# Cross attention: the context is turned on VectorE in 32 by 32 blocks laid out by the transfers, not on TensorE; ScalarE adds the value bias

## What is computed

```
q = (layernorm(x) @ wq.T + bq), k = (ctx @ wk.T + bk), v = (ctx @ wv.T + bv)   # D = 512, 16 heads of 32
scores = q k^T / sqrt(32);  attn = softmax(scores);  ctx_out = attn @ v
x = x + ctx_out @ wo.T + bo
```

## Time and profile before

| | |
|---|---|
| time, median of 3 runs | 1736.51 us (1735.48 to 1738.24) |
| time of the profiled execution | 1736.3 us |
| its span, first to last instruction | 1734.1 us |
| TensorE busy | 1665.6 us, 96% |
| VectorE busy | 1178.3 us, 68% |
| ScalarE busy | 933.3 us, 54% |
| GpSimd busy | 645.9 us, 37% |
| transfers, mean rate | 51 GB/s |

### The profile page before, as it was taken

How to read it: one execution, slowest core, us unless ns; L and a number is a source line. 1 busy time by engine, 2 the same in 40 slices (tenths; PEclk the granted TensorE clock), 3 DMA queues, 4 the chain that set the end, 5 groups by cost and what they waited for, 6 DMA issues and landing times. The chain is left out here.

```text
span 1734.1 us, 37329 instructions
## 1 busy us (share of the span) xinstructions
PE 1665.6 (96%) x16084; PEld 1365.8 (79%) x16084; DVE 1178.3 (68%) x1555; ACT 933.3 (54%) x1405; POOL 645.9 (37%) x352
## 2 busy tenths in 40 slices
PE   7999999999999999999999999868899899999999
PEld 6788888888888888888888888656787677778787
DVE  5137887878788878878787888787633577753322
ACT  4236666666676666666666766654201677731000
POOL 0003555555555555555555545202000144432210
PEclk9999999999999999999999999878899899899999
DMA  5211101011110101010111100213323111211001
GB/s 194 66 42 35 41 30 43 29 41 42 30 42 29 43 29 41 31 43 29 41 38 35 41 29 8 76 47 114 128 85 104 50 56 45 74 51 46 28 25 49
DMA packets 73283, 88.74 MB, mean 51 GB/s; under 512 B 6912, under 2 KB 39680, under 8 KB 73120
## 3 DMA queue, kind: packets, MB, share of 16 engines
q1 hardware_dynamic: 73120, 86.36, 15.5%
HBM read 71.67 MB, written 14.68 MB: 50 GB/s over the span
## 5 line engine op out<-in xcount | busy, mean ns | idle before, releaser
L638 POOL TENSOR_TENSOR b_acc<-b_acc,b_s 128x1024 f32<-128x1024 f32 x168 | 459.0, 2732 | 258.1 <-ACT b_s L846 247.5
L875 DVE TENSOR_TENSOR b_s<-b_s,b_mb 128x2048 f32<-128x2048 f32 x128 | 365.5, 2857 | 3.9 <-ACT b_mb L829 3.9
L913 DVE TENSOR_TENSOR b_mx<-b_psS,b_mx 128x512 f32<-128x512 f32 x480 | 331.1, 690 | 52.4 <-PE b_psS L710 39.2
L846 ACT ACTIVATE b_s<-b_s 128x2048 f32<-128x2048 f32 x128 | 245.2, 1916 | 82.2 <-DVE b_s L875 82.2
L855 ACT ACTIVATE b_s<-b_psS 128x2048 f32<-128x2048 f32 x128 | 240.8, 1881 | 69.7 <-DVE b_mx L913 69.7
L43 PE MATMUL b_work<-wvT,cT 128*128 128x512 f32 x496 | 203.1, 409 | 0.0
L43 PE MATMUL b_work<-cT,wkT 128*128 128x512 f32 x496 | 200.3, 404 | 0.0
L45 PE MATMUL b_work<-wvT,cT 128*128 128x512 f32 x496 | 194.2, 391 | 0.0
L45 PE MATMUL b_work<-cT,wkT 128*128 128x512 f32 x496 | 193.7, 390 | 0.0
L44 PE MATMUL b_work<-wvT,cT 128*128 128x512 f32 x496 | 193.5, 390 | 0.0
L44 PE MATMUL b_work<-cT,wkT 128*128 128x512 f32 x496 | 193.5, 390 | 0.0
(11 more groups left out here) (291 smaller groups left out, 2845.1 us busy)
## 6 DMA issues: line engine op xcount, KB each, us to landing
cin<-in_ctx SPq DMA_DIRECT2D x64, 512.0 KB, 3.4
experts_sb<-in_L_ffn_expert_w SPq DMA_DIRECT2D x8, 1024.0 KB, 5.3
q_scratch<-d_st SPq DMA_DIRECT2D x16, 256.0 KB, 2.3
k_scratch<-d_st SPq DMA_DIRECT2D x16, 256.0 KB, 2.3
e_q<-q_scratch SPq DMA_DIRECT2D x16, 256.0 KB, 2.7
k_sb<-k_scratch SPq DMA_DIRECT2D x16, 256.0 KB, 2.9
b_kT<-in_x SPq DMA_DIRECT2D x4, 512.0 KB, 8.3
q_scratch<-a_q SPq DMA_DIRECT2D x8, 256.0 KB, 2.3
```

The source lines that it names most:

```text
L638: nc.gpsimd.tensor_tensor(acc[:, :, :], acc[:, :, :], s[:, buf, 2 * i:2 * i + 2, :], ALU.add).then_inc(sum_done, 1)
L846: nc.scalar.activation(part, part, ACT.Exp, scale=SCALE).then_inc(exp_done, 1)
L875: nc.vector.tensor_tensor(s[:, n % BUFS, :, :], s[:, n % BUFS, :, :], mb[:, :].rearrange("p (o n) -> p o n", o=1).broadcast_to([P, CHUNK, ...
L913: nc.vector.tensor_tensor(mx[:, :, :], part, mx[:, :, :], ALU.max).then_inc(mx_done, 1)
```

## The change

TensorE no longer turns the context of the chunks 2 to 31. A unit is now 128 features (k) of a chunk of 512 tokens. SP loads it with four transfers, one for each 32 features, each into 32 partitions of `cin`: within a partition lie 16 runs of 32 numbers (128 bytes), so that the 32 x 32 blocks already stand at their final place and only each block has to be turned in itself. VectorE does that with one instruction of 128 x 512 (`nc.vector.transpose`) from one half of `cin` to the other. ScalarE and VectorE then make the high and low half from `cin` in SBUF, where they read PSUM before. A unit is turned in the beat in which the unit before it is split, and its load is issued when the unit two before it has been turned. The turned blocks leave the ring of banks. Apart from that, ScalarE adds the value bias, after the exponential of its beat.

```diff
+def load_blocks(sp, ctx_in, cin, raw_in, p, k):
+    rows = ctx_in[p // 4, (p % 4) * 512:(p % 4 + 1) * 512, k * P:(k + 1) * P]
+    blocks = rows.rearrange("(t j) (i c) -> i j t c", j=32, i=4)
+    for i in range(4):
+        sp.dma_start(cin[32 * i:32 * i + 32, 0, k % 2, :].rearrange("j (t c) -> j t c", c=32),
+                     blocks[i]).then_inc(raw_in[k % 2], 16)
...
+            sp.wait_ge(full, place["c", 1, 1] + 1)
+            for k in range(2):
+                load_blocks(sp, ctx_in, cin, shared.raw_in, 2, k)
...
+            return None if n is None or n < 2 * CHUNK else divmod(n, CHUNK)
+        def turned_next(beat):
+            return transposed(beat + 2)
...
-            if (x0 := transposed(beat)) is not None:
-                enter(("T", *x0), beat)
...
+            sp.wait_ge(turned, 1)
+            load_blocks(sp, ctx_in, cin, shared.raw_in, 2, 2)
             for beat in range(FIRST, LAST):
...
+                if (x0 := turned_next(beat - 1)) is not None and x0[0] * CHUNK + x0[1] + 2 < SLOTS * CHUNK:
+                    u = x0[0] * CHUNK + x0[1]
+                    sp.wait_ge(turned, u - 2 * CHUNK + 1)
+                    load_blocks(sp, ctx_in, cin, shared.raw_in, *divmod(u + 2, CHUNK))
...
             for beat in range(FIRST, LAST):
-                if (x0 := transposed(beat)) is not None:
-                    transposes(*x0)
...
+                    act.wait_ge(turned, (p - 2) * CHUNK + k + 1)
+                    nc.scalar.activation(cT[0][:, p % 2, k, :], cin[:, 1, k % 2, :], ACT.Copy).then_inc(hi_done, 1)
...
+                if (m := normal_slot(beat)) is not None:
+                    g = m % G
+                    act.wait_ge(od_free, m + 1)
+                    if m >= 2:
+                        act.wait_ge(o_out[m % 2], 16 * (m // 2))
+                    nc.scalar.activation(o_st[:, m % 2, :], oq[:, :], ACT.Identity,
+                                         bias=bv[:, g:g + 1]).then_inc(o_done, 1)
...
+            def context_turned(p, k):
+                u = (p - 2) * CHUNK + k
+                dve.wait_ge(shared.raw_in[k % 2], 16 * 4 * (u // 2 + 1))
+                reached(dve, split_done, u - 2 + 2 * CHUNK + 1 if u >= 2 else 0)
+                nc.vector.transpose(cin[:, 1, k % 2, :], cin[:, 0, k % 2, :]).then_inc(turned, 1)
...
+            context_turned(2, 0)
...
-                    nc.vector.tensor_scalar(o_st[:, m % 2, :], oq[:, :], bv[:, g:g + 1], None,
-                                            ALU.add).then_inc(o_done, 1)
...
+                    nc.vector.tensor_tensor(cT[1][:, p % 2, k, :], cin[:, 1, k % 2, :], f32(cT[0][:, p % 2, k, :]),
+                                            ALU.subtract).then_inc(split_done, 1)
+                if (x0 := turned_next(beat)) is not None:
+                    context_turned(*x0)
```

More of the change, by code:

```diff
@@ L119, in __init__ @@
         self.cin_in = [sem(f"cin_in{i}") for i in range(2)]
+        self.raw_in = [sem(f"raw_in{i}") for i in range(2)]
         self.x_in = sem("x_in")
@@ L291, in _ @@
             load_weights(2)
[L292 to L295, removed]
+            for h in range(2):
+                sp.wait_ge(full, place["c", 0, 2 * h + 1] + 1)
+                load_context(1, h)
+            sp.wait_ge(full, place["c", 1, 1] + 1)
+            for k in range(2):
+                load_blocks(sp, ctx_in, cin, shared.raw_in, 2, k)
             for n, (_, half, g) in enumerate(order_of["q"]):
@@ L526, in value_places @@
             return [first + g * step for g in range(G)]
-        ident, cT, v, cin_in = shared.ident, shared.cT, shared.v, shared.cin_in
+        ident, cT, v = shared.ident, shared.cT, shared.v
         wkT, wvT = shared.wkT, shared.wvT
@@ L547, in cross_attention @@
         const = sem("b_const")
+        turned = sem("b_turned")
         bias_in = sem("b_bias_in")
@@ L652, in wait_evicted @@
                     kind, m, n = unit
-                    if kind == "T":
-                        pe.wait_ge(split_done, m * CHUNK + n + 1)
-                    elif kind == "K":
+                    if kind == "K":
                         pe.wait_ge(k_done, m * CHUNK + n + 1)
@@ L666, in bank_of @@
                 return work[BANK[unit]]
[L668 to L677, removed]
             def keys(p, g):
@@ L834, in _ @@
                 if (x0 := transposed(beat)) is not None:
[L835 to L838, removed]
+                    p, k = x0
+                    act.wait_ge(turned, (p - 2) * CHUNK + k + 1)
+                    nc.scalar.activation(cT[0][:, p % 2, k, :], cin[:, 1, k % 2, :], ACT.Copy).then_inc(hi_done, 1)
                 if (m := spread_slot(beat)) is not None:
@@ L879, in _ @@
                 if (m := normal_slot(beat)) is not None:
-                    g = m % G
                     if m == SLOTS - 1:
@@ L892, in _ @@
                     dve.wait_ge(rd_done, m + 1)
+                    reached(dve, o_done, m)
                     nc.vector.tensor_tensor(oq[:, :], psO[:, 0:P], rD[:, :], ALU.mult).then_inc(od_free, 1)
-                    dve.wait_ge(od_free, m + 1)
-                    if m >= 2:
-                        dve.wait_ge(o_out[m % 2], 16 * (m // 2))
-                    nc.vector.tensor_scalar(o_st[:, m % 2, :], oq[:, :], bv[:, g:g + 1], None,
-                                            ALU.add).then_inc(o_done, 1)
-                if (x0 := transposed(beat)) is not None:
-                    p, n = x0
-                    dve.wait_ge(hi_done, p * CHUNK + n + 1)
-                    nc.vector.tensor_tensor(context_place(cT[1], p, n), two(work[BANK["T", p, n]]),
-                                            f32(context_place(cT[0], p, n)), ALU.subtract).then_inc(split_done, 1)
+                if (x0 := transposed(beat)) is not None:
+                    p, k = x0
+                    dve.wait_ge(hi_done, p * CHUNK + k + 1)
+                    nc.vector.tensor_tensor(cT[1][:, p % 2, k, :], cin[:, 1, k % 2, :], f32(cT[0][:, p % 2, k, :]),
+                                            ALU.subtract).then_inc(split_done, 1)
+                if (x0 := turned_next(beat)) is not None:
+                    context_turned(*x0)
                 if (n := score_step(beat)) is not None:
```

1 line of the change is left out of this document (removed).

## The result

The changed kernel takes **1722.13 us** (median of 4 runs, 1721.59 to 1723.19) beside 1736.17 (median of 4, 1735.48 to 1738.24) for the kernel before: a ratio of 0.9916, 95% interval 0.9903 to 0.9928. It is faster by 14.0 us, where 11.6 were forecast (1724.9). The profiled spans are 1734.1 and 1720.6 us, 13.5 apart, so the trace holds nearly all of it.

The account below looks back on a forecast made before the run. TensorE was taken to set the pace of a 34.10 us slot. The first 15 units give 6.5 us, 27 later slots of 0.2 give 5.1: 11.6 off 1736.5, so 1724.9 us (range 1680 to 1742; main case 1714 to 1736).

Parts of the forecast that it names:

- step 3: Chunk 1's split waits for GpSimd's second add, until 19.7 us; chunk 2's scores come at 25.3, TensorE stands still 1.5.
- the circle: The forecast's walk through one steady slot, closing on itself from chunk 3's scores to the next: 33.9 us, 0.2 less.
- step 1: Slot's start: subtraction of the maximum, wanted at 7.98 us, waits for GpSimd's adds until 8.2 and is over at 10.3.
- step 2: Split, turn, maxima and ScalarE's move follow; TensorE starts chunk 1's scores at 16.4 us, with no loss yet.
- step 4: GpSimd's add of chunk 0 holds the split where it held the bias; split over at 28.2 us, scores moved at 33.6.
- step 6: GpSimd's adds of chunk 1 run 28.2 to 33.1 us; the last subtraction ends 1.25 into the next slot.
- The first 15 units: Beats 8 to 36, before GpSimd works in full: TensorE gives back 0.43 us per unit, 6.5 us.
- rival (b): The turn is long and stands twice in the slot's chain: at 1.26 us (two passes) 1759 us; chance 16%.
- (a): The split after chunk 1's scores isn't held by the port: slot 32.4 us, 52 us gained, 1684 us; chance 18%.
- (c): GpSimd's adds fall 0.2 to 0.4 us later than in the circle, eating the gain: 1732 to 1742 us; chance 10%.
- (d): Context transfers are late, above 66 ns per small packet; at 80 ns 216 us more, 1941 us; chance 4%.
- (e): TensorE's clock might be granted at less than full; expected busy 96%, so left out, with no chance given.

Follow-up runs that it names:

- Experiments 1 and 2: GpSimd's adds cut to 8 of 512 columns, most sums left out: in the changed kernel 1688.66 us, in the kernel before 1737.40 us.
- experiment 3: Changed kernel with the split's subtraction (low half of the context) replaced by an equally long instruction with one SBUF input: 1687.38 us.
- experiment 5: Changed kernel with each of GpSimd's adds in two halves of 128x512, all sums kept: 1696.19 us.
- experiment 11: Changed kernel with GpSimd's adds in halves and ScalarE copying the high half one beat earlier for all but a part's first unit: 1696.18 us.
- experiment 4: Changed kernel with every turn made twice, one right behind the other: 1766.32 us.
- Experiment 9: Changed kernel with context loads in rows of 2 KB in place of 128-byte pieces, the layout in blocks left out: 1723.85 us.
- experiment 7: Changed kernel with the value bias back on VectorE: 1725.41 us.
- experiment 10: Changed kernel with GpSimd's adds in quarters of 128x256, same sums: 1696.98 us.

## Why the prediction was right, and where its terms were off

**The port, step 3: right, and shown.** The forecast said that the new split, not the turn, decides the result, since GpSimd's second add has waited and takes the port first. In times from the scores of chunk 3 (560.40), the trace beside the circle:

| event | forecast | measured |
|---|---|---|
| step 1: subtraction over | 10.3 | 570.57: 10.2 |
| step 2: scores of chunk 1 | 16.4 | 576.79: 16.4 |
| step 3: the pair of adds over | 19.2 | 579.51: 19.1 |
| step 3: split over | 19.7 | 579.99: 19.6 |
| step 3: scores of chunk 2 | 25.3 | 585.50: 25.1 |
| step 4: split over | 28.2 | 588.35: 28.0 |
| step 5: scores of chunk 3 | 33.9 | 594.15: 33.75 |

TensorE stands still for 8.71 - 7.38 = 1.3 us, forecast 1.5. Experiments 1 and 2 show that the adds are the cause and only in the changed kernel, 3 that it is the split's second input, 5 that the length of one hold is what counts. Of the Trainium skill (SBUF — State Buffer, "Who interferes with whom") the rule that two SBUF inputs contend and one doesn't agrees with experiment 3 (2.48 against 0.69 at the same place inside the pair of adds); the trace also agrees with its sentence that the shared port is an exclusive lock (the split is over 0.48 us after the add, not before).

**The size of a slot's gain: right in kind, off by half.** Forecast 34.1 to 33.9, measured 34.11 to 33.74: 0.37 in place of 0.2. The circle is 0.15 too long (0.2 with the unrounded 25.3 + 8.65 = 33.95), and all of it lies before the scores of chunk 2, since the 8.65 behind them were exact. About 0.1 is step 1. By step 6 the last subtraction should have ended 1.25 into the next slot; the split at 561.48 shows 1.08. GpSimd's adds for chunk 2 were then over at 563.59 + 4.86 = 568.45, the subtraction at 568.37 met the tail of them and took 2.28, unheld, and through ScalarE's exponential GpSimd's pair of step 3 was over earlier too. The rest is rounding in the chain behind it: from the split's end to the scores of chunk 2 it took 585.50 - 579.99 = 5.51, not 5.6. The sum itself was loose: 27 x 0.2 is 5.4, and with 33.95 it is 27 x 0.15 = 4.1; the recorded 5.1 lies between. With a gain that is the difference of two numbers near 34, 0.15 is nearly its whole size: 5.1 became 9.6.

**The first beats: the wrong term.** "The first 15 units give 15 x 0.43 = 6.5 us" measured 4.0. What failed is the assumption that TensorE alone sets the pace there. Up to the first scores it held: they come at 103.33 in place of 106.33, though TensorE's first instruction of the stage came at 70.48 in place of 70.20. So the 7 units up to there gave 3.3, or 0.47 each. The 8 behind them gave 1.0 in place of 3.4. (Together 4.3, of which the later start takes 0.3.) First TensorE, then VectorE of the changed kernel in those beats:

```profile
103.33 1.17 PE L709 MATMUL b_psS<-b_q,b_kT 32*128 32x128 f32 x32
...
110.81 1.17 PE L709 MATMUL b_psS<-b_q,b_kT 32*128 32x128 f32 x32 [0.63 <-ACT b_s L860]
```

```profile
104.68 0.69 DVE L911 TENSOR_TENSOR cT<-cin,cT 128x512 fp32r<-128x512 f32 x1 [4.12 <-ACT cT L835]
105.29 0.70 DVE L871 STREAM_TRANSPOSE cin<-cin 128x512 f32<-128x512 f32 x1
105.92 0.65 DVE L920 COPY b_mx<-b_psS 128x512 f32<-128x512 f32 x1
```

The scores start at 103.33, but VectorE first waits for the high half, splits and turns, and looks at them only 2.6 us later, at 105.92 (before it was 106.33 to 107.82, 1.5). Of these 1.1 more 0.63 are the turn. The maxima take 2.8 more and ScalarE's move 1.9, and TensorE waits for it, four times among these beats for 0.3 to 0.6 us, 2.0 in total, most of the missing 2.4. TensorE got faster, and the chain of scores, maxima and move took over. The port has no part in it: from the first reduction of turned maxima to the second it is 30.56 us with the adds and 30.54 with the small ones of experiment 1. An early high half (experiment 11) gave only 0.4 us of the 2.4 back, so the split's wait for the high half, ahead of the maxima, is at most a part; how the rest divides stays open. The two misses are of opposite sign (+4.5 and -2.5). That the forecast of 11.6 came as close to 14.0 as it did is luck; its terms were off by more.

**The turn, rival (b): right.** The 120 turns take 695 to 712 ns, and what follows starts 0.63 after their start (105.29 to 105.92). So does the one at 588.35, 0.70 inside a pair of GpSimd's adds (588.23 to 593.15). No second pass over four bytes shows (it would have been 1.26). The Trainium skill's 311 ns for a two-byte 128 x 128 block (VectorE: DVE Perf Modes, "The three transpose paths") can't be held against it: no run here turns two-byte data. The price of a longer turn (0.2 us per slot for 0.1) came out in experiment 4, though by another chain.

**The other rivals.** (a) The split not held: it would have given 1684; the two kernels in which it isn't held gave 1687 and 1689. Its slot, 32.4, was exact, and its 6.5 us for the first beats are most of what is missing. (c) The gain eaten: not here, the adds fell 0.15 earlier than in the circle (568.45 - 560.40 = 8.05, forecast 8.2), not later. Its time of 1732 to 1742 doesn't follow from its own terms either: 0.2 to 0.4 us for each of 27 slots, added to 1724.9, is 1730 to 1736. (d) Transfers: 310240 packets at 21.7% of 16 engines and 1720.6 us are 19 ns each in the mean, far below the 59 of the bound. VectorE waited once for a context load, 1.1 us, at its third turn. Experiment 9 settles it. The warning of the Trainium skill (DMA: Bandwidth & Descriptors, "Specifications") shows in the packets' time and landing, but not in the kernel's. (e) TensorE busy for 96% in the steady window kept a granted clock of 1.00.

**The rest.** The bias on ScalarE takes 0.40 us, shorter than 0.60, as forecast, and costs nobody anything. It also gained less than it seems: step 4 said that the split takes over the bias's wait, and experiment 7 shows that it does, nearly whole. The sync queue issues an output in 0.49 us where it took 0.34; nobody waits for it.

## What to carry to other kernels

Before an operand is moved from PSUM to SBUF, look whether the instruction then has two SBUF inputs, and whether GpSimd works beside it; on such an instruction price the wait for the add that runs and for the one that is queued. If it must stand there, halve GpSimd's instructions: the hold halves, until their fixed cost makes GpSimd itself late. And when the engine that sets the pace gets faster, walk the next chain through stage by stage: here the steady slots and the first beats had different ones.

## What the runs showed of the hardware

- The port goes to whoever has waited: a split that became ready while GpSimd's second add, itself held up, was running waited for all that was left of it, and 0.69 became 2.48. In experiment 11 the split was ready at once behind the subtraction, and the waiting add still went first (1.77). GpSimd is held the same way (an add of 2.40 took 3.46 behind a subtraction that began before it).
- A hold need not cost anything: a subtraction held to 4.53 us in experiment 3 left the slot as short as without the adds, and one of 2.48 in the changed kernel cost TensorE 1.3 of the 1.8 that it was longer.
- VectorE's transpose of four-byte data, 128 x 512 in 32 by 32 blocks, takes 0.70 us, about as long as other instructions of that size here (0.65 to 0.69), and isn't held by GpSimd (0.695 to 0.712 in 120 turns).
- Dividing GpSimd's adds costs a fixed part each time: two of 128 x 1024 take 4.86 us, four of 128 x 512 5.03 (experiment 5, at 619.29), and four of 128 x 256, half the work, 2.80 (experiment 10, at 588.57).
- Loading the context in 128-byte pieces in place of rows of 2 KB raised the queue's share from 16.8% to 21.7% for the same bytes, with 19 ns of an engine per packet in the mean of all; transfers of 64 KB landed after 2.3 us in place of 1.9.
